# Attention of a perceiver layer: scores by row tiles, own keys as a chunk of 33, row sums by ones

## The reference

```python
qkv = (x @ w_qkv.T)                      # 16 heads of 8
k = concat([context keys (257), own keys (32)])      # 289 keys a sequence
v = concat([context values (257), own values (32)])
attn = softmax((q * 8 ** -0.5) @ k.T)    # per sequence and head
out = (attn @ v) @ w_proj.T + b_proj
```

## Time and profile before

| | |
|---|---|
| median of 3 runs | 752.95 us (750.12 to 755.46) |
| profiled execution | 755.94 us, its span 754.2 us |
| PE busy | 622.8 us (83%) |
| DVE, POOL, ACT busy | 465.4, 399.6 and 316.8 us |
| DMA | 33.26 MB, 44 GB/s over the span |

### The profile page before, as it was taken

One profiled execution on the slowest core, in us unless ns is written; L12 is line 12 of the kernel. 1 busy time (PEld: TensorE's weight loads), 2 busy tenths in 40 slices (PEclk: granted clock), 3 DMA queues, 4 the chain that ended last, 5 costly groups with the idle time before them and its releaser, 6 DMA issues. The chain is left out here.

```text
span 754.2 us, 14892 instructions
## 1 busy us (share of the span) xinstructions
PE 622.8 (83%) x4426; PEld 428.6 (57%) x4426; DVE 465.4 (62%) x919; ACT 316.8 (42%) x1003; POOL 399.6 (53%) x685
## 2 busy tenths in 40 slices
PE   3899999999999999997487888889528464777993
PEld 2577777777777777775122222223216254766993
DVE  6077777777777777776628487696654912343446
ACT  3555555655555665552223151504015322343550
POOL 3155555555555555551535849373526666666540
PEclk9999999999999999999559998999956767998997
DMA  5014452121111112110000000000001011111216
GB/s 161 3 44 134 133 133 60 52 56 56 56 56 53 48 54 56 56 42 2 1 0 0 0 1 0 0 1 0 1 0 56 0 29 45 44 40 43 39 37 171
DMA packets 30472, 33.26 MB, mean 44 GB/s; under 512 B 3498, under 2 KB 20996, under 8 KB 30436
## 3 DMA queue, kind: packets, MB, share of 16 engines
q1 hardware_dynamic: 27940, 27.68, 13.0%
q0 software_dynamic: 2496, 5.12, 2.5%
HBM read 28.13 MB, written 4.65 MB: 43 GB/s over the span
## 5 line engine op out<-in xcount | busy, mean ns | idle before, releaser
L594 PE MATMUL psum<-kT,q_heads 128*128 128x289 f32 x512 | 145.9, 408 | 0.8 <-ACT kT L482 0.8
L639 DVE COPY pT<-psum 128x512 f32<-128x512 f32 x128 | 86.5, 676 | 73.3 <-PE psum L554 73.3
L499 ACT ACTIVATE probs<-psum,neg_max 128x289 f32<-128x289 f32 x256 | 126.1, 497 | 12.7 <-DVE inv_sum L672 2.3
L659 DVE TENSOR_REDUCE neg_max<-psum 128x2 f32<-128x578 f32 x128 | 96.7, 755 | 21.8 <-PE psum L594 19.8
L427 POOL TENSOR_TENSOR probs_own<-probs,ones 128x128 f32<-128x128 f32 x64 | 25.8, 404 | 134.9 <-ACT probs L499 134.9
L594 PEld LDWEIGHTS psum<-kT,q_heads 128*128 128x128 f32 x512 | 87.3, 190 | 16.1 <-issue 1.0
L554 PE MATMUL psum<-ident,probs 128*128 128x128 f32 x512 | 79.0, 277 | 0.9 <-ACT probs L499 0.8
L554 PEld LDWEIGHTS psum<-ident,probs 128*128 128x128 f32 x512 | 64.3, 152 | 11.3 <-ACT probs L499 1.6
L395 POOL TENSOR_TENSOR q_heads<-qT,head_scaled 128x512 f32<-128x512 f32 x64 | 67.2, 1050 | 6.1 <-ACT k_own L469 6.1
L479 ACT COPY pT_own<-psum 128x128 f32<-128x128 f32 x64 | 17.0, 266 | 119.6 <-PE psum L545 119.6
L836 POOL TENSOR_TENSOR read<-recep,state 128x496 f32<-128x496 f32 x32 | 44.7, 1397 | 39.6 <-DVE state L1058 39.6
(11 more groups left out here) (257 smaller groups left out, 1320.0 us busy)
## 6 DMA issues: line engine op xcount, KB each, us to landing
kv_in<-in_ctx SPq DMA_DIRECT2D x64, 256.0 KB
w_gate<-in_L_ffn_Wg SPq DMA_DIRECT2D x1, 1408.0 KB, 7.5
w_up<-in_L_ffn_Wu SPq DMA_DIRECT2D x1, 1408.0 KB, 6.7
x_res<-in_x SPq DMA_DIRECT2D x4, 256.0 KB, 3.7
v_left_in<-in_ctx SPq DMA_DIRECT2D x64, 2.0 KB
w_down<-in_L_ffn_Wd SPq DMA_DIRECT2D x2, 512.0 KB, 5.2
x_rows<-x_cen SPq DMA_DIRECT2D x4, 256.0 KB, 2.3
w_gate<-y_rows SPq DMA_DIRECT2D x4, 256.0 KB, 3.7
```

The source lines that it names most:

```text
L499: last = nc.scalar.activation(probs[:, par, gr, :], bank[S_BANK[h][k]][:, 0:KEYS], ACT.Exp, bias=neg_max[:, par, gr:gr + 1], accum_out=row ...
L594: last = pe.matmul(bank[S_BANK[h][k]][:, 0:KEYS], q_heads[:, par, HG * gr:HG * gr + HG, :].rearrange("p h n -> p (h n)"), kT[:, par, :], s ...
L639: nc.vector.tensor_copy(pT[:, par, h, :], bank[PT_BANK[h]][:]).then_inc(s_pT_out, 1)
L659: nc.vector.tensor_reduce(neg_max[:, par, 2 * h:2 * h + 2], psum[:, 2 * h:2 * h + 2, 0:KEYS], AX.X, ALU.max, negate=True).then_inc(s_max, 1)
```

## The change

The attention step is rewritten.

- `q_heads` has 128 columns in place of 512. A group's scores use the 32 partitions of its own channels for weights and keys. The two groups of a pair use different partitions and write to different banks. Own keys and the 257th context key are the last 33 of the 289.
- Own values and the 257th value lie in 33 rows of one buffer (`v_own`), for even sequences from partition 0, for odd ones from 64. `turn_own` turns the last 33 (or 97) probabilities of each group (four transposes), between the first and second half of the values. The row sums come from products whose weights are ones. So `values` has 24 products 32 columns wide: 12 with the values and 12 with ones; a third of these take 33 rows, the others 128.
- Keys are turned two sequences ahead, the values formed two behind; keys and values have slots and transfers of their own.
- ACT no longer sums rows; it copies the first half of the turned probabilities and the result rows. DVE copies the second half and the own part. POOL masks and sums the result (three instructions), and scales it behind DVE's reciprocal.
- Own values are projected by 16 products for each 512 rows, before by 64, and DVE shares their copies. Two transfers put the 257th value into `v_own`, and the transpose of `k_left` waits for them too.
- Eight steps are written out ahead of the loop, and eight behind it. `NXS` is 12. Semaphores that nothing used are gone.

```diff
-    for u in range(NSLOT):
-        step(u, u)
-    with eng.Fori(1, B // NSLOT - 1) as turn:
+    for b in range(PEELED * NSLOT):
+        step(b, b % NSLOT)
...
+    left_rows = ctx_dram[:, NCTX - 1, C:2 * C].rearrange("(i r) c -> r i c", r=2)
+    for r in range(2):
+        sp.dma_start(v_own_pairs[64 * r + N:64 * r + 2 * N, :, :],
+                     left_rows[r:r + 1, :, :].broadcast_to([N, B // 2, C])).then_inc(s_left_in, 16)
...
+    def load_keys(b, u):
+        if not first(b, NSLOT):
+            sp.wait_ge(s_keys, b - NSLOT + 1)
+        sp.dma_start(k_in[:, u, :, :], rows_of(b, slice(0, C))).then_inc(s_k_in[u], 16)
+    def load_values(b, u):
         if not first(b, NSLOT):
             sp.wait_ge(s_pv, b - NSLOT + 1)
...
+        sp.dma_start(v_in[:, u, :, :], rows_of(b, slice(C, 2 * C))).then_inc(s_v_in[u], 16)
...
-        g.tensor_tensor(q_heads[:, par], qT[:, queries_of(b)].unsqueeze(1).broadcast_to([P, H, N]),
-                        head_scaled[:].unsqueeze(2).broadcast_to([P, H, N]), ALU.mult)
+        g.tensor_tensor(q_heads[:, par], qT[:, queries_of(b)].unsqueeze(1).broadcast_to([P, HG, N]),
+                        head_in_group_scaled[:].unsqueeze(2).broadcast_to([P, HG, N]), ALU.mult)
...
+    def ready_v(b, u):
+        if first(b, 1):
+            pool.wait_ge(s_v_own, NB)
+            pool.wait_ge(s_v_own_odd, NB)
+            pool.wait_ge(s_left_in, 48)
+        if not first(b, 4):
+            pool.wait_ge(s_pv, b - 2)
+        g.tensor_copy(v_now[:, u // 2, :], v_own[:, bass.ds(b * (C // 2), C)]).then_inc(s_ready_v, 2)
+    def normalise(b, par):
+        pool.wait_ge(s_o_rows, b + 1)
+        g.tensor_tensor(o_masked[:], o_rows[:, par].rearrange("p s (h n) -> p s h n", h=HG),
+                        head_in_group[:].unsqueeze(1).unsqueeze(3).broadcast_to([P, 2, HG, N]),
+                        ALU.mult).then_inc(s_o_steps, 1)
+        pool.wait_ge(s_o_steps, 2 * b + 1)
+        g.tensor_tensor(o_pairs[:], o_masked[:, :, 0:HG // 2, :], o_masked[:, :, HG // 2:HG, :],
+                        ALU.add).then_inc(s_o_steps, 1)
+        pool.wait_ge(s_o_steps, 2 * b + 2)
         if not first(b, 2):
...
+            pool.wait_ge(s_attn, b - 1)
+        g.tensor_tensor(o_sum[:, par], o_pairs[:, :, 0, :], o_pairs[:, :, 1, :], ALU.add).then_inc(s_o_sum, 1)
+    def attended(b, par):
+        pool.wait_ge(s_o_inv, b + 1)
+        g.tensor_tensor(attn_T[:, queries_of(b)], o_sum[:, par, 0, :], o_inv[:, par, :], ALU.mult).then_inc(s_attn, 1)
...
+        par = u % 2
+        if exists(b + 1):
+            ready_q(b + 1, 1 - par)
+        if exists(b) and par == 0:
+            ready_v(b, u)
+        if exists(b - 4):
+            attended(b - 4, par)
+        if exists(b - 3):
+            normalise(b - 3, 1 - par)
...
+    def rows_out(b, par):
+        act.wait_ge(s_pv, b + 1)
+        if not first(b, 2):
+            act.wait_ge(s_o_steps, 2 * b - 3)
+        nc.scalar.copy(o_rows[:, par], O_BANK[:, 0:2 * P].rearrange("p (s q) -> p s q", s=2)).then_inc(s_o_rows, 1)
+    def probs_out(b, par):
+        act.wait_ge(s_pT0, b + 1)
+        if not first(b, 2):
+            act.wait_ge(s_pv, b - 1)
+        nc.scalar.copy(pT[:, par, 0, :], bank[PT_BANK[0]]).then_inc(s_pT0_out, 1)
     def step(b, u):
         par = u % 2
...
+        if exists(b - 3):
+            rows_out(b - 3, 1 - par)
+        if exists(b - 1):
+            probs_out(b - 1, 1 - par)
+        if exists(b + 2):
+            act.wait_ge(s_scores, 2 * b + 2)
+            keys_out(b + 2, par)
+        if exists(b):
+            for h in range(2):
+                act.wait_ge(s_max, 2 * b + (h + 1))
+                if h == 0 and not first(b, 2):
+                    act.wait_ge(s_own_T, b - 1)
+                for k in range(2):
+                    gr = 2 * h + k
+                    last = nc.scalar.activation(probs[:, par, gr, :], bank[S_BANK[gr]][:, 0:KEYS], ACT.Exp,
+                                                bias=neg_max[:, par, gr:gr + 1])
+                last.then_inc(s_exp, 1)
...
-    pe.wait_ge(s_kleft_in, 16)
+    pe.wait_ge(s_left_in, 48)
...
+        for half in range(2):
+            if n:
+                pe.wait_ge((s_v_own, s_v_own_odd)[half], n)
+            for i in range(TPB):
+                for r in range(2):
+                    at = BLK * n + N * (2 * (TPB * half + i) + r)
+                    last = pe.matmul(bank[4 + half][64 * r:64 * r + N, C * i:C * i + C], ln_T[:, at:at + N],
+                                     w_T[:, 2, :], start=True, stop=True, skip_group_check=True)
+            last.then_inc(s_proj, 1)
...
+    def turn_own(b, par):
+        start = KEYS - (N + 1) - 64 * par
+        for gr in range(G):
+            last = pe.transpose(KEY_BANK[0:KEYS - start, P * gr:P * gr + P], probs[:, par, gr, start:KEYS], ident[:])
+        last.then_inc(s_own_T, 1)
...
+        if par == 0:
+            pe.wait_ge(s_ready_v, b + 2)
+        pe.wait_ge(s_v_in[u], loaded(b, u))
+        pe.wait_ge(s_pT0_out, b + 1)
+        pe.wait_ge(s_pT1_out, b + 1)
+        pe.wait_ge(s_own_out, b + 1)
+        mine = own_rows(par)
+        for s in range(2):
+            for c in range(KC):
+                if s == 0 and c == 1 and between:
+                    between()
+                for gr in range(G):
+                    rows = slice(N * gr, N * gr + N)
+                    pe.matmul(O_BANK[rows, P * s:P * s + P],
+                              ones[:] if s else v_in[:, u, c, rows],
+                              pT[:, par, gr // 2, P * (2 * (gr % 2) + c):P * (2 * (gr % 2) + c) + P],
+                              start=(c == 0), stop=False, skip_group_check=True)
             for gr in range(G):
                 rows = slice(N * gr, N * gr + N)
...
+                last = pe.matmul(O_BANK[rows, P * s:P * s + P],
+                                 ones[mine, :] if s else v_now[mine, u // 2, rows],
+                                 pT_own[mine, P * gr:P * gr + P],
+                                 start=False, stop=True, skip_group_check=True)
...
+    def scores(b, par, h):
+        pe.wait_ge(s_ready_q, b + 1)
+        pe.wait_ge(s_keys_out, b + 1)
+        if first(b, 1):
+            pe.wait_ge(s_k_own, NB + 1)
+            pe.wait_ge(s_ln_T, NB)
+        else:
+            pe.wait_ge(s_exp, 2 * b + (h - 1))
+        for gr in (2 * h, 2 * h + 1):
+            rows = slice(N * gr, N * gr + N)
+            last = pe.matmul(bank[S_BANK[gr]][:, 0:KEYS],
+                             q_heads[rows, par].rearrange("p h n -> p (h n)"),
+                             kT[rows, par, :], start=True, stop=True)
+        last.then_inc(s_scores, 1)
...
+        par = u % 2
+        if exists(b):
+            scores(b, par, 1)
+        if exists(b + 2):
+            keys(b + 2, (u + 2) % NSLOT)
+        if exists(b - 1):
+            pe.wait_ge(s_exp, 2 * b)
+            if not first(b, 2):
+                pe.wait_ge(s_pT1_out, b - 1)
+            elif b == 1:
+                pe.wait_ge(s_v_own_odd, NB)
+            turn_probs(b - 1, 1 - par, 1).then_inc(s_pT1, 1)
+        if exists(b - 1) and exists(b - 2):
+            pe.wait_ge(s_keys_out, b + 3 if exists(b + 2) else B)
+            values(b - 2, (u + 2) % NSLOT, par, lambda: turn_own(b - 1, 1 - par))
+        elif exists(b - 1):
+            pe.wait_ge(s_keys_out, b + 3)
+            turn_own(b - 1, 1 - par)
+        elif exists(b - 2):
+            values(b - 2, (u + 2) % NSLOT, par)
+        if exists(b + 1):
+            pe.wait_ge(s_exp, 2 * b + 1)
+            scores(b + 1, 1 - par, 0)
+        if exists(b):
+            pe.wait_ge(s_exp, 2 * b + 1)
+            if first(b, 1):
                 pe.wait_ge(s_v_own, NB)
...
             else:
...
+                pe.wait_ge(s_pT0_out, b)
+            turn_probs(b, par, 0).then_inc(s_pT0, 1)
...
+        if exists(b - 1):
+            v.wait_ge(s_pT1, b)
+            if not first(b, 3):
+                v.wait_ge(s_pv, b - 2)
+            nc.vector.tensor_copy(pT[:, 1 - par, 1, :], bank[PT_BANK[1]]).then_inc(s_pT1_out, 1)
+            v.wait_ge(s_own_T, b)
+            mine = own_rows(1 - par)
+            nc.vector.tensor_copy(pT_own[mine, :], KEY_BANK[mine, :]).then_inc(s_own_out, 1)
+        if exists(b - 3):
+            v.wait_ge(s_o_sum, b - 2)
+            if not first(b, 5):
+                v.wait_ge(s_attn, b - 4)
+            nc.vector.reciprocal(o_inv[:, 1 - par, :], o_sum[:, 1 - par, 1, :]).then_inc(s_o_inv, 1)
...
-NXS = 15
+NXS = 12
```

More of the change, by code:

```diff
@@ L439, in step @@
-                    if not first(b, 1):
-                        spread(b - 1, (u + 1) % 2)
-                for u in range(NSLOT):
-                    step(u, u)
+                    par = u % 2
[7 more added lines that the diff above has]
+                        normalise(b - 3, 1 - par)
@@ L444, in _ @@
+                for b in range(PEELED * NSLOT):
+                    step(b, b % NSLOT)
                 pool.wait_ge(s_qT, NB)
```

(47 more changed lines are left out.)

291 lines of the change are left out of this document (80 added, 211 removed).

## The result

| | us |
|---|---|
| predicted | 780 (740 to 812), slower with 0.62 |
| the change, median of 4 runs | 821.84 (809.03 to 824.98) |
| the kernel before beside it, median of 4 runs | 751.54 (748.84 to 755.46) |
| ratio | 1.0834, 95% interval 1.0681 to 1.0987 |
| profiled execution, span | 818.3 (before 754.2) |

The ratio uses fast runs alone: for the change these are 809.03 and 820.03 us, one on each side of the range's upper end, and the other two are over 1.5% above the fastest.

What follows compares the result with a forecast made beforehand. PE was taken as the bound: a step of 5.31 us, 0.41 more, gives +26.2 over 64 sequences; with tail +1.4, front +1.4 and +1.6, experts -3.8, +26.8 on 755.94, 783, less 3.0 for the median: 780 us (740 to 812).

Steps and rivals of the forecast that it cites:

- The likeliest case: Whole kernel: the forecast itself, an attention step of 5.31 us and a time of 780 us (770 to 795), chance 0.45.
- the wait for ACT's copy of the keys: Attention step, ahead of the values: PE waits 0.08 us for ACT to finish copying the keys.
- Streaming, 3.81: Attention step on PE: pure streaming takes 3.81 us, some 0.4 below before, with scores running two at a time.
- Rival 3: Attention scores: pairs overlap only in part, +0.49 us a step and 811 us, chance 0.13.
- Ten changes, 1.42: Attention step on PE: ten changes of tile form cost 1.00 us in drains and 0.42 in fills.
- The drain: Attention step on PE: each change of tile form costs 0.10 us of draining, 1.00 for ten.
- the fills: Attention step on PE: weights not loaded ahead across changes of form cost 0.42 us a step.
- Rivals 1 and 2: Attention step: changes of row form alone are free (757 us, chance 0.17); transposes pay nothing (726 us, chance 0.18).
- The tail, +1.4: End of attention: 1.42 us before the output projection become near 2.8 through a copy, four POOL steps and a reciprocal.
- The front, +3.0: Ahead of attention: +1.4 us for waiting on two more transfers (ends 0 and 3.5), +1.6 for projecting own values.
- The own values' 1.6: Projection of own values ahead of attention: about 0.4 us more, four times, from 32 records in two column tiles.
- The experts, -3.8: Experts: three fewer gathers at 1.25 us end an idle gap 3.8 us earlier (ends 0 and -3.8).

Runs made afterwards that it cites:

- e7: The change with e4's and e5's edits, each step reordered to all scores, then all transposes, then all products: 664.1 us, 0.919 of the kernel before.
- e2: The change with PE's wait for ACT's copy of the keys moved inside the values, ahead of their fourth product: 1.064 of the kernel before.
- e5: e1 and e4 together, with own products and own ones reading all 128 rows, zeros in the other rows: 1.025 of the kernel before.
- e1: The change with the wait for ACT's copy of the keys placed last of PE's waits ahead of the values: 1.062 of the kernel before.
- e10: e4 plus fourteen transposes of the identity while PE waits for the first exponentials: 1.072 of the kernel before.
- e8: The kernel before with 12 tiles in place of 15 for the experts' gathered rows: 0.999 of the kernel before.
- e4: The change with the left value rows' transfers waited for by POOL alone, not ahead of the left keys' transpose: 1.081 of the kernel before.
- e9: e6 plus eight identity transposes ahead of the first scores and ten while PE waits for the first exponentials: 714.4 us, 0.988 of the kernel before.
- e6: The kernel before with only its scores put in row tiles (32 rows per group): 940.6 us, 1.300 of the kernel before.
- e3: The change with all 64 sequences' steps written out, no loop on PE, ACT, DVE and POOL: 1.064 of the kernel before.

## Why the prediction was wrong

The sign and the mechanism stood: streaming falls by 0.4 us a step and ten changes of form take more than that back. The likeliest case had 0.45, and its account of streaming and forms is the one that the runs bear out, but its sum was 37 us short. More than half of that, 20 us, is one term, the wait for ACT's copy of the keys. Step by step:

- **Streaming, 3.81: right.** The pair takes one group's time; e7 shows the same for four groups. Rival 3 is refuted: four records of 0.244 are through in 0.49 and the form's 0.20. It rested on a reading of the rule quoted with it, that products start and end strictly in order (the Trainium skill, TensorE: Matmul & The Clock Gate, Part 3). Taken for single records, as rival 3 took it, the rule does not fit here. Taken for whole products it does: the pair's records start at 200.842 and 200.849, then at 201.189 and 201.196, and the last two end 0.007 us apart.
- **Ten changes, 1.42: 1.52 measured (e2).** 0.10 a step, 6 us. The drain is 0.09 at each of the ten changes of e2's step, those that change rows alone too, so what the sum had too small is the fills, 0.60 in place of 0.42. Rivals 1 and 2 are refuted: the first by e5, the second by the 0.12 to 0.17 that every group of transposes pays. Here the trace agrees with the Trainium skill, TensorEngine Tiling (Array Packing), Key Properties.
- **The wait for ACT's copy of the keys, 0.08: this is the step that failed.** It was measured as 0.45 in the loop (5.78 less 5.33) and 0.16 where steps are written out (5.49 less 5.33), in all 20 us more than the sum had. The copy itself came when I had it: in e1 PE starts 0.05 behind its end, and the wait there is 0.10. What I missed is what stands behind the wait in PE's queue. The first of six or seven waits ended last; in the loop the others, with the registers that hold their values, came behind it at about 0.1 us each, and nothing hid them. In the kernel before, show a start 0.05 behind the copy, and I carried that over.
- **The clock, not in the sum: 5.2 us** (e10). The output projection takes 1.7 more, with the granted clock at 0.50 from 415 to 422 us, where it was 1.00 before. That the 2.83 us of idle time ahead of it are the cause is not shown: in e8 the idle time is the 1.01 us of the kernel before, and yet the clock is 0.57 there from 352 to 356 us and the projection takes 1.2 longer than before. The prediction asked what PE waits for, but not at which clock it comes back.
- **The tail, +1.4: +5.6.** From the start of the last products to the projection it is 3.25 (412.89 to 416.14) against 1.42, so 1.8 for the 1.4 of the sum. The other 3.8 are the values two behind, which leave two sequences' values behind the last maximum. At the start the same lag gives 3.3 back: the first two steps have no values (2.72 and 3.79 in e10, 3.59 and 5.43 before).
- **The front, +3.0: +6.4.** The wait for two transfers costs 5.7 (e4), beyond my end of 3.5, which had them at 303 GB/s with nothing else under way. The own values' 1.6 is at most 0.7 at the first maximum. PE's projections, up to the first keys, take 16.6 us in e4 and 15.3 in the kernel before, but 16.4 in e8, whose front is the same.
- **The experts, -3.8: +0.9.** e8 refutes the cause I named. The gap was read as a cost of the gathers ahead of it, but it moves.
- Between the start of the time mixing and the first gather 3.9 us went away (253.0 to 249.0). It need not belong to the change: in the experiments, whose code is the same there, this stretch takes 244.7 to 248.7 us, and e4 and e10 differ by 3.6. Why stays open.

The sum of the measured parts in the two profiles: 6.4 front, 53.4 from first to last maximum (25.8 for 63 steps of +0.41, 20 wait, 6 forms, 5.2 clock, -3.3 at the start), 5.6 tail, 1.7 projection, -3.9, 0.9: 64.1.

## What to carry to other kernels

Count changes of TensorE's tile form before streaming. Ten of them took 1.52 us a step, where row tiles save 0.98, and the same operations sorted by form, with the edits of e4 and e5 (e7), beat both kernels. When a wait is moved or added, read what stands behind it in its engine's queue, and put the one that ends last at the end, above all in a loop whose waits hold registers. Look at the granted clock in the first steps of a stage: work put into the gap at its start brought back 5 us in one kernel (e10) and 226 in another (e9 against e6).

## What was not expected of the hardware

- A loop can hold either clock. e6 and e9 have the same loop; in e6 the granted clock fell to 0.50 near 37 us and stayed there for 520 us, with PE shown as busy throughout, and in e9 it was 1.00 to the end of the attention. Step 8.36 against 4.76, four runs within 937 to 942 us, ten within 711 to 722.
- Waits that are already over are not free when their values are in registers and they stand behind the one that ends last: 0.29 us a step for the change's own (5.78 less the 5.49 of e3), at about 0.1 us from one record of PE's sequencer to the next. Where they stand ahead of it (e1), PE starts 0.05 us behind the copy.
- Products over 33 rows are dearer than the same over 128 rows with zeros if their neighbours have 128: the three changes of rows in a step cost 0.40 us (e5).
